# The first state-space scan of a twelve-layer kernel, spread over the units of the attention layer ahead of it

## What is computed

```
x = _layernorm(x + _L0_attn_ref(x, ...))               # layer 0, causal attention, 16 heads of 16
x = _layernorm(x + _L0_xattn_ref(ctx_1024, x, ...))    # layer 1, state-space scan
...
x = _layernorm(x + _L1_xattn_ref(ctx_1024, x, ...))    # layer 4, the same with other weights

# _xattn_ref(hidden_states = ctx, z = x):
u = silu(conv(in_proj @ ctx) + conv_b);  dt_low, B, C = x_proj @ u
delta = softplus(dt_proj @ dt_low + dt_b);  A = -exp(A_log)     # 256 channels, 16 states
def step(state, (d, b, c, u)):
    state = state * exp(d * A) + (d * u) * b;  return state, state @ c
y = scan(step, 0, ...) + D * u
return y * silu(z)
```

## Time and profile before

| | us |
|---|---|
| median of 3 runs | 2671.76 (2666.47 to 2681.22) |
| profiled execution | 2666.48, its span 2664.5 |
| PE busy | 1977.8 (74%) |
| DVE busy | 1610.6 (60%) |
| ACT busy | 786.8 (30%) |
| POOL busy | 580.7 (22%) |

### The profile page before, as it was taken

How to read it: one execution, slowest core, us unless ns; L and a number is a source line. 1 busy time by engine, 2 the same in 40 slices (tenths; PEclk the granted TensorE clock), 3 DMA queues, 4 the chain that set the end, 5 groups by cost and what they waited for, 6 DMA issues and landing times.

```text
span 2664.5 us, 27749 instructions
## 1 busy us (share of the span) xinstructions
PE 1977.8 (74%) x9734; PEld 1251.4 (47%) x9734; DVE 1610.6 (60%) x2456; ACT 786.8 (30%) x1999; POOL 580.7 (22%) x327
## 2 busy tenths in 40 slices
PE   5646668746635776788888864553999999999986
PEld 3522234412222445666666633343566665555743
DVE  4279956879988543555555179998366424444114
ACT  1333302133212025455554011110355314444000
POOL 1314420014501014233332036555000000000000
PEclk9867878768867879888889877876899999999966
DMA  3000020010010210000001100000000100000000
GB/s 102 7 32 0 0 54 3 5 45 0 0 40 1 35 42 2 17 12 12 12 10 50 71 1 0 0 0 0 6 10 10 42 10 13 12 10 21 1 32 16
DMA packets 25727, 48.98 MB, mean 18 GB/s; under 512 B 6262, under 2 KB 19603, under 8 KB 24092
## 3 DMA queue, kind: packets, MB, share of 16 engines
q1 hardware_dynamic: 25644, 47.85, 5.9%
HBM read 42.20 MB, written 1.05 MB: 16 GB/s over the span
## 4 chain that ended last, share of the span: by engine, by line
PE 51%; DVE 37%; ACT 4%; issue 4%; SPq 1%; POOL 1%; DMA 1%; DVEq 0%; ACTq 0%; POOLq 0%
DVE big L795 8%; PE banks L1116 7%; PE banks L1085 7%; PE banks L1125 7%; PE banks L1054 6%; DVE big L1796 5%; PE banks L1108 3%; DVE big L1792 3%; DVE big L495 2%; PE banks L1350 2%; PE banks L417 2%; PE banks L428 2%; DVE big L790 2%; DVE big L776 1%; DVE arena L1172 1%
## 5 line engine op out<-in xcount | busy, mean ns | idle before, releaser
L1191 DVE COPY arena<-banks 128x512 f32<-128x512 f32 x196 | 135.4, 691 | 329.8 <-PE banks L1108 329.5
L218 POOL TENSOR_TENSOR ln_rstd<-ln_var_eps,neg_half 128x2 f32<-128x2 f32 x48 | 36.8, 766 | 1060.8 <-DVE ln_var_eps L206 1060.8
L1085 PE MATMUL banks<-big 128*128 128x256 f32 x784 | 235.6, 413 | 6.0 <-ACT big L1227 4.4
L1116 PE MATMUL banks<-arena,big 128*128 128x256 f32 x784 | 227.7, 414 | 6.3 <-DVE arena L1191 6.3
L1248 ACT ACTIVATE arena<-banks,arena 128x256 f32<-128x256 f32 x392 | 193.0, 499 | 60.8 <-DVE arena L1165 43.0
L795 DVE TENSOR_TENSOR_SCAN big<-big 128x2048 f32<-128x2048 f32 x32 | 204.2, 6380 | 1.1
L707 PE MATMUL banks<-big,ident 128*128 128x512 f32 x288 | 171.3, 749 | 39.2 <-POOL big L868 39.1
L868 POOL TENSOR_TENSOR big<-big 128x2048 f32<-128x2048 f32 x32 | 144.7, 4523 | 252.2 <-DVE big L795 252.2
L1266 ACT ACTIVATE big<-banks 128x256 f32 (+1 forms) x196 | 75.1, 383 | 348.4 <-PE banks L1116 348.4
L1054 PE MATMUL banks<-x_feat,arena 128*128 128x512 f32 x392 | 176.4, 592 | 0.0
L1125 PE MATMUL banks<-arena,big 128*128 128x256 f32 x784 | 174.3, 382 | 1.9 <-ACT big L1266 1.9
(11 more groups left out here) (313 smaller groups left out, 3568.1 us busy)
## 6 DMA issues: line engine op xcount, KB each, us to landing
big<-big SPq DMA_DIRECT2D x32, 64.0 KB, 2.3
arena<-in_L0f_w SPq DMA_DIRECT2D x1, 2048.0 KB, 8.0
arena<-in_L1a_wo SPq DMA_DIRECT2D x1, 2048.0 KB
arena<-in_L1f_gv SPq DMA_DIRECT2D x1, 2048.0 KB
arena<-in_L2a_qk_w SPq DMA_DIRECT2D x1, 2048.0 KB
big<-big SPq DMA_DIRECT2D x64, 32.0 KB
arena<-in_L2x_wo SPq DMA_DIRECT2D x1, 2048.0 KB
arena<-in_L2x_q_w SPq DMA_DIRECT2D x16, 128.0 KB, 2.0
```

The lines of the kernel that those rows point to most:

```text
L1085: last = mm(ps[:, h * SEQ:(h + 1) * SEQ], q[:, b * SEQ + h * P:b * SEQ + (h + 1) * P], k[:, b * SEQ:(b + 1) * SEQ], start=True, stop=not s ...
L1116: last = mm(slot, self.v[:, 2 * b + kc, :], self.probs_t[:, u % 2, kc, :], start=(kc == 0), stop=(kc == 1))
L1191: v.tensor_copy(self.probs_t[:, u % 2].rearrange("p a b -> p (a b)"), B[4 + u % 2][:]).then_inc(self.turn_read, 1)
```

## The change

- StateSpace is cut into functions (`tensor_in`, `tensor_low`, `tensor_dt`, `tensor_slot`, `vector_slot` and so on). A step is now one state of two sequences: 32 steps of 2 x 512 = 1024 words a partition, written out instead of a loop. Both layers 1 and 4 use it.
- A step's drive is made by GpSimd from a copy of B in SBUF in 20 of 32 steps, and by VectorE from PSUM in 12 (`driver`). B and C of a step stand in banks 4 and 5 and are copied by one ScalarE instruction (C alone where VectorE drives). The copies (`bc`), decay, drive, state and out have two buffers each.
- Outputs are added in token order: `out` is the weight operand and the identity the moving one, eight fp32 products of 128 columns a step into banks 6 and 7 (`tensor_add`). D*u is added in the same way behind the last state of each half, so that no transposes follow. ScalarE copies y to SBUF.
- The gate's Silu moves into the activation with which the LayerNorm before fills x_feat; in its last part the layer multiplies y with it, and its LayerNorm reads y from SBUF.
- Layer 1's instance is hosted by layer 0. Its weights are loaded there, its projections and convolution run between those of the attention, one softplus instruction follows the reductions of each of units 0 to 10, one step each follows units 11 to 15, and 27 steps stand in the second pass, two, two and one to a unit. The attention has one slot of four banks instead of two, its last transposes use two pairs of banks by turns instead of four, and its mask in the second pass is a PE product (`score_t`) instead of GpSimd's `affine_select`.
- Layer 4's instance runs by itself in the new form. Layer 6, the other SmallHeads, hosts nothing and keeps two slots.

```diff
@@ -232,7 +236,7 @@
         for pair in range(TILES // 2):
             act.wait_ge(e.xt_psum, 4 * l + pair + 1)
             nc.scalar.activation(e.x_feat[:, :, pair * D:(pair + 1) * D],
-                                 e.bank[4 + pair][:].rearrange("p (c t) -> p c t", c=CH), ACT.Copy).then_inc(e.xt_ready, 1)
+                                 e.bank[self.turn_bank(pair)][:].rearrange("p (c t) -> p c t", c=CH), ACT.Silu if self.gates else ACT.Copy).then_inc(e.xt_ready, 1)
 
     def sync(self, sp):
         pass
...
+        return self.stage.rearrange("p s k t -> p (s k t)")
+
+    def first_slots(self, u):
+
+        at = u - StateSpace.SOFTPLUS
+        return range(at, at + 1) if self.hosts and at >= 0 else ()
+
+    def second_slots(self, u):
+
+        first = self.units - StateSpace.SOFTPLUS
+        upto = lambda n: min(first + n // 3 * 5 + n % 3 * 2, STEPS)
+        return range(upto(u), STEPS if u == self.units - 1 else upto(u + 1)) if self.hosts else ()
+
+    def slot(self, u):
+        return 4 * (u % self.slots)
...
+            for n in self.first_slots(u):
+                self.beside.tensor_slot(pe, n)
         turn_max(G - 1)
 
         def score_t(u):
...
+                blocks = B[slot + j][:, 0:3 * P].rearrange("p (a b) -> p a b", b=P)
+                mm(blocks[:, 0:3:2, :], e.causal_bf[:, P:2 * P], bcast(e.ident_bf[:], 1, 2), start=True, stop=False, skip_group_check=True)
             for kc in range(2):
                 for j in range(4):
                     rows = self.rows(j)
                     last = mm(B[slot + j][:, kc * SEQ:kc * SEQ + (2 - kc) * P], self.k[rows, g, b * SEQ + kc * P:b * SEQ + (kc + 1) * P],
-                              self.q[rows, g, b * SEQ + kc * P:(b + 1) * SEQ], start=True, stop=True, skip_group_check=True)
+                              self.q[rows, g, b * SEQ + kc * P:(b + 1) * SEQ], start=masked, stop=True, skip_group_check=True)
             last.then_inc(self.scored_t, 1)
...
+        if not self.hosts:
+            score_t(0)
         for u in range(self.units):
-            if u + 1 < self.units:
-                score_t(u + 1)
+            if u + self.slots - 1 < self.units:
+                score_t(u + self.slots - 1)
+            for n in self.second_slots(u):
+                self.beside.tensor_slot(pe, n)
             sum_up(u)
 
...
+            for n in self.second_slots(u):
+                self.beside.vector_slot(dve, n)
             dve.wait_ge(self.summed, u + 1)
             nc.vector.tensor_copy(self.out_t(g)[:, b * SEQ:(b + 1) * SEQ].rearrange("p (h t) -> p h t", h=2),
                                   e.banks[:, slot:slot + 2, 3 * P:4 * P]).then_inc(self.sum_read, 1)
 
         for g in range(G):
...
+
+        for u in range(self.units):
+            if u % 4 == 0 and u:
+                read_max(u // 4 - 1)
+            for n in self.first_slots(u):
+                if n == 0:
+                    self.beside.scalar_step(act, 0)
+                self.beside.scalar_slot(act, n)
+        read_max(G - 1)
...
+            for n in self.second_slots(u):
+                self.beside.scalar_slot(act, n)
         if self.diff:
...
@@ -582,6 +669,16 @@
             pool.wait_ge(self.w_loaded, self.n_loads)
             e.wait_x_tok(pool, self.l)
             nc.gpsimd.tensor_tensor(e.x_tok[:], e.x_tok[:], bcast(self.proj_b, 1, TILES), ALU.add).then_inc(self.x_biased, 1)
+        for u in range(self.units):
+            for n in self.first_slots(u):
+                if n == 0:
+                    self.beside.gpsimd_drive(pool, 0)
+                self.beside.gpsimd_slot(pool, n)
+        if self.hosts:
+            for u in range(self.units):
+                for n in self.second_slots(u):
+                    self.beside.gpsimd_slot(pool, n)
+            return
         zero = pool.to_reg(0.0)
         for u in range(self.units):
             for n in range(2):
...
+    def driver(self, k):
+
+        return "dve" if k % 8 in (2, 5, 7) else "pool"
+
+    def driven(self, eng, k):
+
+        who = self.driver(k)
+        eng.wait_ge(self.s_driven[who], sum(self.driver(n) == who for n in range(k + 1)))
...
+    def tensor_spread(self, pe, k):
+        if k == 0:
+            pe.wait_ge(self.s_parts, 2)
+        else:
+            pe.wait_ge(self.s_bc_read, k)
+            if self.driver(k - 1) == "dve":
+                self.driven(pe, k - 1)
+        for n in range(2):
+            last = self.e.nc.tensor.matmul(self.e.bank[4 + n][:], self.pick[0:3 * BC, n * STATES + k % STATES, :], self.parts[0:3 * BC, self.cols(k)], start=True, stop=True)
+        last.then_inc(self.s_bc_psum, 1)
...
+    def tensor_add(self, pe, k):
+        e = self.e
+        first, last = k % STATES == 0, k % STATES == STATES - 1
+        if k == 0:
+            pe.wait_ge(self.s_dt_act, 4)
+        elif first:
+            pe.wait_ge(self.s_y_read, k // STATES)
+        pe.wait_ge(self.s_outed, k + 1)
+        sources = [self.out[:, k % 2]] + ([self.u[:, :, self.cols(k)]] if last else [])
+        for src in sources:
+            if src is not sources[0]:
+                pe.wait_ge(self.s_skip, k // STATES + 1)
+            for t in range(4):
+                for j in range(CH):
+                    at = (t % 2) * D + j * P
+                    ins = e.nc.tensor.matmul(e.bank[6 + t // 2][:, at:at + P], src[:, j, t * P:(t + 1) * P], e.ident[:],
+                                             start=(first and at == 0), stop=False, skip_group_check=True)
+            if src is sources[0]:
+                ins.then_inc(self.s_added, 1)
+            else:
+                ins.then_inc(self.s_y_psum, 1)
+
+    def tensor_slot(self, pe, s):
+        if s + 1 < STEPS:
+            self.tensor_spread(pe, s + 1)
+        if s:
+            self.tensor_add(pe, s - 1)
...
+    def vector_softplus(self, dve, i):
+
+        v, ch = self.e.nc.vector, self.e.dve_chain
         y, acc = self.tiny, self.delta
-        dve.wait_ge(self.s_delta, 4)
-        ch.link(dve, v.tensor_scalar(acc, y, LOG1P[-1], None, ALU.mult))
-        for c in LOG1P[-2::-1]:
-            ch.link(dve, v.scalar_tensor_tensor(acc, acc, c, y, ALU.add, ALU.mult))
-        v.tensor_tensor(acc, acc, self.du, ALU.add).then_inc(self.s_delta_dve, 1)
-        dve.wait_ge(self.s_delta_dve, 1)
...
+    def vector_drive(self, dve, k):
+        if self.driver(k) == "dve":
+            dve.wait_ge(self.s_du, 1)
+            dve.wait_ge(self.s_bc_psum, k + 1)
+            if k >= 2:
+                dve.wait_ge(self.s_scanned, k - 1)
+            self.e.nc.vector.tensor_tensor(self.drive[k % 2], self.du[:, :, self.cols(k)], bcast(self.e.bank[4][:], 1, CH), ALU.mult).then_inc(self.s_driven["dve"], 1)
+
+    def vector_slot(self, dve, s):
+        if s + 1 < STEPS:
+            self.vector_drive(dve, s + 1)
+        dve.wait_ge(self.s_cleared, 1)
+        dve.wait_ge(self.s_decay, s + 1)
+        self.driven(dve, s)
+        if s >= 2:
+            dve.wait_ge(self.s_outed, s - 1)
+        flat = lambda ap: ap.rearrange("p j t -> p (j t)")
+        self.e.nc.vector.tensor_tensor_scan(flat(self.state[:, s % 2]), flat(self.decay[:, s % 2]), flat(self.drive[s % 2]), 0.0,
+                                            ALU.mult, ALU.add).then_inc(self.s_scanned, 1)
+
...
+    def scalar_step(self, act, k):
+        a, n = self.e.nc.scalar.activation, k % STATES
+        if k == 0:
+            act.wait_ge(self.s_cleared, 1)
+            act.wait_ge(self.s_delta, 1)
+            self.e.act_chain.join(act)
+        else:
+            act.wait_ge(self.s_scanned, k - 1)
+        for j in range(CH):
+            seqs = lambda ap: ap.rearrange("p (b t) -> p b t", b=2)[:, :, 1:]
+            last = a(seqs(self.decay[:, k % 2, j, :]), seqs(self.delta[:, j, self.cols(k)]), ACT.Exp, scale=self.a_neg[:, j, n:n + 1])
+        last.then_inc(self.s_decay, 1)
+        act.wait_ge(self.s_bc_psum, k + 1)
+        if k >= 2:
+            act.wait_ge(self.s_outed, k - 1)
+        first = self.driver(k) == "dve"
+        a(self.bc[:, k % 2, first:, :], self.e.banks[:, 4 + first:6, :], ACT.Copy).then_inc(self.s_bc_read, 1)
...
+    def gpsimd_drive(self, pool, k):
+        if k == 0:
+            pool.wait_ge(self.s_du, 1)
+            self.e.nc.gpsimd.memset(self.decay.rearrange("p k j (b t) -> p (k j b) t", t=SEQ)[:, :, 0:1], 0.0).then_inc(self.s_cleared, 1)
+        if self.driver(k) == "pool":
+            pool.wait_ge(self.s_bc_read, k + 1)
+            if k >= 2:
+                pool.wait_ge(self.s_scanned, k - 1)
+            self.e.nc.gpsimd.tensor_tensor(self.drive[k % 2], self.du[:, :, self.cols(k)], bcast(self.bc[:, k % 2, 0, :], 1, CH), ALU.mult).then_inc(self.s_driven["pool"], 1)
+
+    def gpsimd_slot(self, pool, s):
+        if s + 1 < STEPS:
+            self.gpsimd_drive(pool, s + 1)
+        pool.wait_ge(self.s_bc_read, s + 1)
+        pool.wait_ge(self.s_scanned, s + 1)
+        if s >= 2:
+            pool.wait_ge(self.s_added, s - 1)
...
```

(9 more changed lines are left out.)

435 lines of the change are left out of this document (236 added, 199 removed).

## The result

| | before | after |
|---|---|---|
| median | 2673.11 (2666.47 to 2681.22, 4 runs) | 2710.16 (2705.20 to 2715.45, 4 runs) |
| profiled execution, its span | 2666.48, 2664.5 | 2705.20, 2703.5 |

The ratio is 1.0134, with a 95% interval of 1.0108 to 1.0161: the change costs 37 us. The forecast was 2760: the sign came true and the size did not, +37 in the medians and +39 in the profiles where +88 stood.

What follows compares the result with a forecast made beforehand. VectorE's scan and GpSimd's products were taken to exclude each other, so their sum sets the step. Second scan layer +59, table load +1 and hosted layers +28 made +88 on the profiled 2666.5, forecast 2760 us, range 2700 to 2845.

Steps and rivals of the forecast that it cites:

- The exclusion of scan and GpSimd product: Scan loops: VectorE's scan and a GpSimd product never overlap, whichever starts first blocks the other; old step 4.29 + 4.53 = 8.9 us.
- The rival that products of 1024 overlap freely: Scan steps: 1024-element products do not exclude the scan, 4.6 us a half step in layer 4, kernel 2649; chance 0.05.
- The order in the step: Layer 4's half step: out product precedes the waiting scan after a GpSimd drive; after a VectorE drive scans follow directly; 6.4 us average.
- scan first: After a GpSimd drive the waiting scan precedes the out product; 7.9 us a half step in layer 4, kernel 2829; chance 0.14.
- The price of GpSimd's product: New scan step: a GpSimd product of 1024 elements takes 2.2 to 2.3 us, as half of the old 4.52.
- only the port counts: Only the scan/GpSimd exclusion limits steps: 5.8 us a half step in layer 4, hosted part at its fast end, 2695; chance 0.08.
- The hosted layers: Layers 0 and 1 with hosting: second LayerNorm at 393 us instead of 364.8, +28; ends -19 and +90.
- The forecast's chain through the unit's sum: Hosted second pass: in-order queues chain out, add, sum, copy, score and drive; 7.4 us a half step, 200 in all.
- The clock rival (+55): PE stays at 1.2 GHz through the whole hosted part, +55 us, kernel 2815; chance 0.14.
- the clock term: Hosted second pass: PE at 2.4 GHz for 0.62 of the time, weighting 14.2 and 17.8 us per two half steps to 15.6.
- The rest of the program: Everything outside the two scan layers and the hosting attention layer: untouched, 0 us change.
- Tail of layer 4: Behind layer 4's last scan: two rounds of sums, ScalarE copy, product and hand-overs to the LayerNorm, 7.2 us.

Runs made afterwards that it cites:

- the hosting run: Changed kernel with layer 4 put back to the earlier kernel's StateSpace class, so only the first scan layer is hosted and new; 2683.97 us, ratio 1.0057.

## Why the prediction was right or wrong, point by point

**The exclusion of scan and GpSimd product: right.** It was read from the earlier trace rows at 2048 elements and holds at 1024 in both directions (3.90 for a held scan, 3.84 for a held product). The rival that products of 1024 overlap freely is out. The Trainium skill, "SBUF — State Buffer", section "Who interferes with whom", says that a VectorE instruction with two SBUF inputs contends with a GpSimd instruction that reads SBUF, and calls the contention an exclusive lock. The trace agrees: of the held scan's 3.90 us 2.14 lie behind the end of GpSimd's product, and of the held product's 3.84 us 1.79 lie behind the end of the scan.

**The order in the step: right.** Out before scan behind a GpSimd drive, two scans in a row and a bare ScalarE copy behind a VectorE drive. The rival "scan first" did not occur in the steady state.

**The price of GpSimd's product: the step that failed.** It is a mis-sized term of the sum. The prediction said 2.2 to 2.3, "since L868 has the same operands as the new out product". It has not: L868 read both inputs from `big`, the new one reads B or C from the arena. That was in the diff and in the rows, which print `big<-big` for the one and `big<-big,arena` for the 1.94 of L1285, the row that I named the low end and passed over. Measured, 2.00, for the drive and for the out. In the half step the drive came to 1.79 behind the scan, the out to 2.0, and scan, drive and out to 5.9 instead of 6.7; two half steps with a VectorE drive among them mostly to 11.27 instead of 12.6; the mean over 24 is 5.79 instead of 6.4. The loop from the first scan to the last out was 182.3 instead of 204. That is 21.7 of the 49 us of error between +88 and +39, and the run with both products made slow again puts 17 of them back (198.9 from the first scan to the last out); its median is 20 higher. The forecast's end of 5.8 was the right number for a wrong reason: it stood there for "only the port counts".

The page that the prediction named has the same price. The Trainium skill, "GPSIMD Engine Reference", section 3.1, gives about 2.6 cycles an element for a two-input product, an estimate of 2.2 us for 1024. The traces agree where both inputs lie in one buffer (2.33) and do not where they lie in two (2.00); the measurement decides.

**The hosted layers: mechanism right in the main, size off by 18.** Forecast +28, seen +10.5. The first scan was to start at 127 and did at 123.5; the second pass at 164.5 and did at 154.5, mostly because units 12 to 15 with the row maxima took 31.0 and not 37.5, in which a half step was to cost 7.5. The pass itself took 196.8 to the last sum copy against 200, and the stretch from there to the second LayerNorm 23.9 against 28.5. The forecast's chain through the unit's sum held the pass: putting the sum ahead took 27 off. The clock rival (+55) is out: 0.78 was granted in the pass. That is near the 0.81 that the forecast's weights come to, so the clock term was about right.

**The rest of the program: the third mis-sized term.** It was put at zero without a reason beyond "untouched". It held +5 to +6 at the end of layer 3 by an earlier fall of the clock, less 15.6 in layers that nobody touched. The first is against the kernel and the second for it; without them the change would have cost +49 in the profile, and of the 15.6 nothing is explained beyond the granted clock.

**Tail of layer 4: right.** 7.1 against 7.2. The start of 7.1 was forecast as 2.6, and the clock's earlier fall ahead of it accounts for the difference, by the 5.7 of the hosting run; the first scan waits for decay, copy and drive in line, 4.71 of idle before it.

**The sum.** In medians, hosting alone is +17 and the new step in layer 4 the other 20 to 26 (37 less 17; 2710 less 2684). In the profiles the errors are -17.5 (hosted), -21.1 (layer 4 from its first scan), +5.3 (ahead of that scan) and -15.6 (untouched layers): -49 of +88.

## What to carry to other kernels

Two engines that exclude each other at memory set a step by the sum of their instructions, so moving a product onto the second of them costs what it adds. The ways out seen here are an input that is not in SBUF (VectorE's drive with B in PSUM took 1.21 to 1.22 throughout) and a cheaper product. When a price is taken from a row, compare the operands by their buffers and not only by their shape. And when work is threaded into an in-order queue, look first at what the host's own next step waits for, and put that ahead.

## What was not expected of the hardware

- GpSimd's elementwise product is priced by where its inputs lie: 2048 elements took 4.52 with both in `big` and 3.81 with one in an arena; 1024 took 2.33 and 2.00. By the difference of the two sizes that is 2.14 and 1.77 ns an element. Moving the copy within `big` changed nothing.
- TensorE's granted clock in unchanged layers was 0.88 and 0.99 in one kernel and 0.83 and 0.95 in another, up to 15.6 us on 1900, with identical instructions. So a difference of 0.5% between two builds of such a program can be the clock alone. Why it differs stays open.
- The fp32 sums with the identity, 2.05 at 2.4 GHz and 3.78 at 1.2 GHz for 16 records, set 12 of layer 4's 31 intervals between scans once GpSimd was relieved (14 were long, and 2 of them stayed with half of the sums). PE waited a third of that time, and the granted clock was 0.81.
